# A transformer block's attention output written with heads and queries exchanged, in place of a query split that exchanged them

## What is computed

```
x = x + layernorm(attention(layernorm(x)))     # 32 query heads, 8 key/value heads of 128, causal
x = x + layernorm(ffn(layernorm(x)))           # silu(g) * u, inner width 1792

# attention, for key/value head k and its 4 query heads g
scores = einsum('bskgd,btkd->bkgst', qh, kh) * scale
scores = where(causal, scores, min)
probs  = softmax(scores)
attn   = einsum('bkgst,btkd->bskgd', probs, vh).reshape(B, S, 32 * 128)
out    = attn @ w_dense.T
```

## Time and profile before

| | |
|---|---|
| median of 3 runs | 1152.4 us |
| the profiled execution, its own time | 1152.48 us |
| its span, first to last instruction | 1150.7 us |
| mean granted TensorE clock | 0.991 |
| busy in the span: PE, DVE, ACT, POOL | 1100.3, 858.5, 665.7, 827.9 us |
| DMA | 227.9 MB |

### The profile page before, as it was taken

How to read it: one execution, slowest core, us unless ns; L and a number is a source line. 1 busy time by engine, 2 the same in 40 slices (tenths; PEclk the granted TensorE clock), 3 DMA queues, 4 the chain that set the end, 5 groups by cost and what they waited for, 6 DMA issues and landing times.

```text
span 1150.7 us, 16547 instructions
## 1 busy us (share of the span) xinstructions
PE 1100.3 (96%) x5134; PEld 912.6 (79%) x5134; DVE 858.5 (75%) x1706; ACT 665.7 (58%) x1231; POOL 827.9 (72%) x821
## 2 busy tenths in 40 slices
PE   8999999999999999998999999999999899999997
PEld 7888888888888787777877777877888677888885
DVE  5545455557999898899889998888677866566666
ACT  6432324239897687777777877865577532222224
POOL 7844447449979879798789699897865656666545
PEclk9999999999999999999999999999999999999999
DMA  6444565445997898797887988976210033333422
GB/s 222 125 169 146 183 203 185 148 124 195 328 349 264 287 308 303 271 321 238 288 299 241 317 317 268 331 272 214 100 65 1 14 120 105 116 102 99 119 66 96
DMA packets 163536, 227.86 MB, mean 198 GB/s; under 512 B 37760, under 2 KB 126464, under 8 KB 158592
## 3 DMA queue, kind: packets, MB, share of 16 engines
q1 hardware_dynamic: 163456, 226.88, 59.4%
HBM read 130.50 MB, written 96.34 MB: 197 GB/s over the span
## 4 chain that ended last, share of the span: by engine, by line
PE 51%; POOL 16%; DVE 11%; DMA 11%; ACT 5%; issue 5%; SPq 1%; DVEq 0%; POOLq 0%; ACTq 0%
PE psOY L1598 14%; PE psS L1598 14%; PE psT L1598 12%; PE psOY L1735 5%; PE psOY L1750 4%; POOL pT_lo L673 4%; DMA p_scr_short<-probs_short 3%; POOL probs_long L733 3%; DMA p_scr_long<-probs_long 3%; POOL qT_lo L673 3%; DMA squares_long<-p_scr_long 2%; POOL probs_short L733 2%; DVE pT_lo L1254 2%; PE psT L1716 2%; DVE squares_long L1341 1%
## 5 line engine op out<-in xcount | busy, mean ns | idle before, releaser
L1048 ACT ACTIVATE probs_long<-probs_long,negmax 128x896 f32<-128x896 f32 (+9 forms) x124 | 122.2, 987 | 25.1 <-DVE negmax L1322 24.5
L733 POOL TENSOR_SCALAR probs_long<-probs_long,rsum 128x768 f32<-128x768 f32 (+9 forms) x98 | 104.0, 1068 | 35.5 <-DVE rsum L1329 35.2
L673 POOL TENSOR_TENSOR pT_lo<-squares_long,pT_hi 128x896 fp32r<-128x896 f32 (+3 forms) x47 | 105.8, 2257 | 16.3 <-ACT pT_hi L1043 16.3
L1341 DVE STREAM_TRANSPOSE squares_long<-squares_long 128x1792 f32<-128x1792 f32 (+3 forms) x54 | 101.7, 1886 | 17.5 <-DMA squares_long<-p_scr_long 17.4
L1750 PE MATMUL psOY<-wd_hi,oT_hi 128*128 128x512 f32 x256 | 105.7, 413 | 8.8 <-DVE oT_lo L1254 7.7
L673 POOL TENSOR_TENSOR qT_lo<-q_raw,qT_hi 128x512 fp32r<-128x512 f32 x64 | 102.6, 1604 | 11.6 <-ACT qT_hi L1032 11.6
L800 POOL TENSOR_SCALAR hidden<-mask,hr,hs 128x128 f32<-128x128 f32 x112 | 50.4, 459 | 80.9 <-DVE hr L1419 78.7
L1735 PE MATMUL psOY<-pT_hi,v_hi 128*128 128x512 f32 x222 | 89.9, 405 | 15.9 <-POOL pT_lo L673 10.0
L1750 PE MATMUL psOY<-wd_lo,oT_hi 128*128 128x512 f32 x256 | 101.5, 397 | 0.0
L1750 PE MATMUL psOY<-wd_hi,oT_lo 128*128 128x512 f32 x256 | 101.5, 396 | 0.0
L1598 PE MATMUL psS<-kT_hi,qT_hi 128*128 128x512 f32 (+5 forms) x280 | 98.6, 352 | 2.9 <-DVE negmax L1322 1.9
(11 more groups left out here) (214 smaller groups left out, 3386.8 us busy)
## 6 DMA issues: line engine op xcount, KB each, us to landing
q_raw<-q_scr SPq DMA_DIRECT2D x64, 256.0 KB, 4.7
p_scr_long<-probs_long SPq DMA_DIRECT2D x14, 896.0 KB, 7.0
squares_long<-p_scr_long SPq DMA_DIRECT2D x14, 896.0 KB, 5.7
p_scr_long<-probs_long SPq DMA_DIRECT2D x12, 1024.0 KB, 5.9
squares_long<-p_scr_long SPq DMA_DIRECT2D x12, 1024.0 KB, 6.5
p_scr_long<-probs_long SPq DMA_DIRECT2D x14, 768.0 KB, 4.9
squares_long<-p_scr_long SPq DMA_DIRECT2D x14, 768.0 KB, 5.1
raw<-in_w_qk SPq DMA_DIRECT2D x10, 1024.0 KB, 6.4
```

What stands on the lines that cost most here:

```text
L673: return nc.gpsimd.tensor_tensor(dst, source, hi.bitcast(F32), ALU.subtract)
L733: nc.gpsimd.tensor_scalar(row, row, rsum[:, column(t, u)], 1.0, ALU.mult, ALU.mult).then_inc(p_ready[lane(t)], 1)
L1048: nc.scalar.activation(row, row, ACT.Exp, bias=negmax[:, column(t, u)], scale=-1.0, accum_out=lsum[:, column(t, u)]).then_inc(e_done[lane( ...
L1341: nc.vector.transpose(rows, rows).then_inc(swap_turned[c], 1)
```

## The change

For exchanged tiles, the query split no longer reorders: `from_units(qT) <- by_head(q_raw)` for every tile. In an exchanged tile's unit the row is now head-major, partition 32b + q, the exchange makes it (a, b, s) with q = 4s + a, and psO comes out so. The copy of the output undoes what concerns the heads (`turned_rows`) and leaves the tokens of a unit in the order (a, s) in place of (s, a). Tiles that are not exchanged must bring their tokens into the same order; a copy with that many dimensions is written as four, one for each head.

So the rows of `y` and `x1` are permuted tokens. `tokens_of` gives the matching rows in DRAM, for one unit at a time: the loads of x and the stores of the result become four transfers each. The means of x, which DVE holds by tokens in order, go through a DRAM tensor `m_scr` and come back permuted in `xmv`. The mask of the exchanged tiles (`band`) is copied from the other mask. All five letter strings are new; in each only the order differs (of PE's the first line is shown).

```diff
-    PE_WEAVE = ("pspsppssvvvvsppsyysppysppyvppssvspspvvppvvvbbsbsbvbssyybyyvvvssbyyyybssvvvvvvvbbssyvyyyvssbvybvbyvbvvyyv"
+    PE_WEAVE = ("ppspspssvvvvppsspspypypvsppssysppsyvvpsspvvbbvvvbbssyyyyvvvsbbsyybbyybsbsvvvvvvvssyvybyyvbbssbvvvyvyyvyv"
...
-        def queries_in(tile, t):
+        def turned_rows(t):
 
             if away(t):
-                return tile[:].rearrange("p (u q b) -> p u q b", u=HG, b=HG)
-            return from_units(tile)
-
-        def queries_of(tile, t):
-            return tile[:].rearrange("p (b u q) -> p u q b", u=HG, b=HG) if away(t) else by_head(tile)
+                tiles = [u[:].rearrange("p (b w s) -> p b w s", b=HG, s=TURN_ROWS) for u in oT]
+                return [(psO.rearrange("p (w b s) -> p b w s", b=HG, s=TURN_ROWS), *tiles)]
+            banks, tiles = psO.rearrange("p (u b s a) -> p b u a s", u=HG, b=HG, a=HG), [
+                u[:].rearrange("p (b u a s) -> p b u a s", b=HG, u=HG, a=HG) for u in oT]
+            return [(banks[:, h], *[u[:, h] for u in tiles]) for h in range(HG)]
+
+        def tokens_of(t, i, u):
+
+            return t[i * P + u * SPAN:i * P + (u + 1) * SPAN, :].rearrange("(s a) d -> a s d", a=HG)
...
+                    sp.dma_start(m_scr, mv[:].rearrange("p i k -> p (i k)")).then_inc(mean_out, 16)
...
+                    sp.wait_ge(mean_out, 16)
+                    for u in range(HG):
+                        sp.dma_start(xmv[u * SPAN:(u + 1) * SPAN].rearrange("p i k -> p (i k)"), tokens_of(m_scr, 0, u)
+                                     ).then_inc(mean_in, 16)
...
-                        sp.dma_start(x1[:, i, :], x[i * P:(i + 1) * P, :]).then_inc(x_in[i], 16)
+                        for u in range(HG):
+                            sp.dma_start(x1[u * SPAN:(u + 1) * SPAN, i, :], tokens_of(x, i, u)).then_inc(x_in[i], 16)
...
-                sp.dma_start(out[i * P:(i + 1) * P, :], x1[:, i, :]).then_inc(out_done, 16)
-            sp.wait_ge(out_done, 16 * NT)
+                for u in range(HG):
+                    sp.dma_start(tokens_of(out, i, u), x1[u * SPAN:(u + 1) * SPAN, i, :]).then_inc(out_done, 16)
+            sp.wait_ge(out_done, 16 * HG * NT)
...
-                hi, lo = (queries_in(u, t) for u in qT[t % 3])
-                low(lo, queries_of(q_raw[t % 2], t), hi).then_inc(q_lo, 1)
+                hi, lo = (from_units(u) for u in qT[t % 3])
+                low(lo, by_head(q_raw[t % 2]), hi).then_inc(q_lo, 1)
...
-                nc.scalar.copy(queries_in(qT[t % 3][0], t), queries_of(q_raw[t % 2], t)).then_inc(q_hi, 1)
+                nc.scalar.copy(from_units(qT[t % 3][0]), by_head(q_raw[t % 2])).then_inc(q_hi, 1)
...
-                    nc.scalar.copy(by_head(oT[0]), from_units(psO)).then_inc(o_hi, 1)
+                    for bank, hi, _ in turned_rows(args[0]):
+                        last = nc.scalar.copy(hi, bank)
+                    last.then_inc(o_hi, 1)
...
-                    lo_part(by_head(oT[1]), from_units(psO), by_head(oT[0])).then_inc(o_done, 1)
+                    for bank, hi, lo in turned_rows(args[0]):
+                        last = lo_part(lo, bank, hi)
+                    last.then_inc(o_done, 1)
```

More of the change, by code:

```diff
@@ L74, in sandwich_kernel @@
     SPAN = P // HG
+    TURN_ROWS = SPAN // HG
     AWAY = range(3, T - NT)
@@ new lines, in sandwich_kernel @@
+    ACT_WEAVE = ("pppepeeqeppoqppeepprepqeqpeenpeepnpqpffroeffeeqeqohhffqfrfeeeqkeorhhffofeefnqkeeqnohffhqffoeekqeeknohnhf"
+             "ofqfqfkeekeerohrhffoqffeeqkerehohffreeoffkneenqffohfqfheeoqnkeekqohnhqoeffkeffeekqohfhfroffeqreeeqkhohff"
+             "freeofkrnqeeqnffohhfqfoekeqeeknohnffhfoeeqfekkeqrohhrffreeoqffkeerohhqffeefonfqkqeeffnohhffoqeekknoheeqf"
+             "nfhffoeeqeekkqohhofrfffeerqrkeeorqhffhffoqeeekeqnffohhnqoffeekkonqeenhohqfefefqfkekeohffffrhoqrerekreefo"
+             "fqhfhfqeeokqneeffnffohhqoeefkqfnkeeohnfheofqerkkeerohhqoferefffeeqkohqhqoekeereohhoqeeeppoppepopqpppeppe"
+             "eepaeeoppqpcpeeopiapppeepjeqaepcppceieeopepjepoppippapeppeeeopapcpepejppipepaoppcxcijxoixgaxjcgjxaigcjxi"
+             "gtgxjgxtgdttdgdtd")
@@ new lines, in sandwich_kernel @@
+    POOL_WEAVE = ("bnnqnnqdnqrnnnnqnqdmrmmmnnqnnqllmmmmqrnnnnqllmmnmmqqnlmqmrmmqnnkldlmmqmmqnnknnrllqrmmmmnnnndlqlmmmmnrnqm"
+             "qmlmrmqnnkqllqdmmmmnnnnqklrlrmmmmnnqnnqdmmllmmnqqrnrlmqmmmqnknldmlmnmnmqkqnnrlmmlmqmnnrdnnqlmmlmmnqrqnmm"
+             "mmrlqnklndmqmlmmnqnknndlmlrmqmmrqnnnnqmmllmmrqrqnnlmmmmqnkqdnllmmmmqnnknnlmmlmmrrqnnqnnmmqllmmnqqrrmmnmm"
+             "qldnkqnlmlmnqmnmrknnllqrmmnnmmnqrnllqqlnndrnnndnnqnununnzynqunnaqnnyxuynnaunnxannnnuqxnynnnaynnxnnyaaxwx"
+             "ygawgyxagwgxgwgwgwg")
@@ L297, in sandwich_kernel @@
         st = small("st", [P, 2, 6])
-        mv = small("mv", [P, NT, 2])
+        mv, xmv = small("mv", [P, NT, 2]), small("xmv", [P, NT, 2])
         rstd, rstd1, nmean = (small(n, [P, NT]) for n in ("rstd", "rstd1", "nmean"))
@@ L333, in sandwich_kernel @@
         LENGTHS = ("short", "long")
-        swap_out = [[sem(f"swap_out_{n}{k}") for k in range(HG)] for n in LENGTHS]
-        swap_in = [[sem(f"swap_in_{n}{k}") for k in range(HG)] for n in LENGTHS]
+        swap_out = [[sem(f"swap_out_{n}{k}") for k in range(HG // 2)] for n in LENGTHS]
+        swap_in = [[sem(f"swap_in_{n}{k}") for k in range(HG // 2)] for n in LENGTHS]
         swap_turned, swap_hi, swap_lo, swap_lo_pool = ([sem(f"{what}_{n}") for n in LENGTHS] for what in
                                                        ("swap_turned", "swap_hi", "swap_lo", "swap_lo_pool"))
+        mean_out, mean_in = sem("mean_out"), sem("mean_in")
         wd_in, ffn_in, out_done, ffn_free = sem("wd_in"), sem("ffn_in"), sem("out_done"), sem("ffn_free")
@@ L498, in swap_away @@
                     sp.wait_ge(swap_in[c][k], 16 * (count - 2))
-                by_quarter = kept(t, k).rearrange("(b p x) -> p b x", b=HG, p=P)
-                sp.dma_start(by_quarter, rows.rearrange("p (b x) -> p b x", b=HG)).then_inc(swap_out[c][k], 16)
+                scratch, width = kept(t, k)
+                by_quarter = scratch.rearrange("(b p x) -> p b x", b=HG, p=P)
+                sp.dma_start(by_quarter[:, :, 0:width], rows.rearrange("p (b x) -> p b x", b=HG)).then_inc(swap_out[c][k], 16)
             def swap_back(t, k):
@@ L509, in swap_back @@
                         sp.wait_ge(swap_lo_pool[c], low_count(earlier, POOL_LOW, end))
-                sp.dma_start(rows, kept(t, k).rearrange("(p x) -> p x", p=P)).then_inc(swap_in[c][k], 16)
+                scratch, _ = kept(t, k)
+                sp.dma_start(rows, scratch.rearrange("(p x) -> p x", p=P)).then_inc(swap_in[c][k], 16)
             def store(kind, n, tile, done):
@@ L953, in _ @@
                     corner = band[:, HG - 1, 2 * P - SPAN:2 * P]
-                    nc.gpsimd.affine_select(out=corner, in_=corner, compare_op=ALU.is_ge, fill=NEG, base=0,
-                                            pattern=[[-HG, SPAN]], channel_multiplier=1).then_inc(band_ready, 1)
+                    nc.gpsimd.tensor_scalar(corner, mask[:, S - SPAN:S], 1.0, 1.0, ALU.mult, ALU.mult).then_inc(band_ready, 1)
                 elif kind == "zeros":
```

62 lines of the change are left out of this document (27 added, 35 removed).

## The result

The changed kernel takes **1137.1 us** (median of 4 runs, 1132.85 to 1137.74) against 1152.2 for the kernel before (4 runs): a ratio of 0.9856, 95% interval 0.9823 to 0.989, or 13 to 20 us less. The prediction was 1154 with a range from 1146. It missed, and by a part that it had given nothing: the new orders. (One run of the kernel before, beside e13 to e16, took 1542.3 us at a granted clock of 0.655; it is left out of all comparisons.)

A forecast was written before the change was run, and what follows sets the result against it. TensorE's own work was taken to bound the kernel, leaving its idle time to win (31.8 us in the attention stage). Query split -9, output's copy +1.5, stores +9 sum to +1.5 on 1152.48, so 1154 us, range 1146 to 1161.5.

The forecast's parts named there:

- The orders: New order of the engines' instructions: nothing in a row tells what they are worth, so no term in the sum.
- a bad new order: Risk named, without a size: a new order that leaves TensorE waiting where it didn't would make the prediction wrong.
- an attention stage that gains over 15 us: Sign named beforehand that would show the prediction wrong; the attention stage was expected to gain about 9 us.
- The query split: Attention stage, 53 exchanged tiles: splitting without reordering frees ACT 27.9 us and POOL 19.0; taken as -9 us, bounds 0 and -19.
- The output's copy: Copy from PSUM: nothing for exchanged tiles, four instructions per engine for 11 others; taken as +1.5 us, bounds 0 and 16.
- The stores: End of kernel: four transfers per tile, each quarter on four DMA engines, 2.6 us per tile; taken as +9 us.
- The loads of x: 32 issues on SP from 821.5, holding four DMA engines 21 us in the worse case; covered, so no cost.
- the margin of 2 to 5 us: Time by which the x loads were expected to stay covered before the cast at 847.1, in the worse case.
- DVE sets the pace: Rival: the change gives DVE nothing between 250 and 850; -2 in the attention stage, sum +8.5, 1161 us, chance 0.20.
- More is won: Rival: in the attention stage whatever POOL is given back shows up, -16 there, sum -5.5, 1147 us, chance 0.17.
- Spread stores: Rival: the final stores use all DMA engines, costing +4.7 us in place of +9; 1149.6 us, chance 0.15.
- dear reads: Rival: strided reads in the output's copy are dear, half of 16 us exposed, +8 for +1.5; 1160 us, chance 0.08.

The follow-up runs named there:

- e13: Kernel before with its own orders, from tile 20 on POOL subtracts only two of four parts of each low part of the exchanged probabilities: 1132.6 us.
- e16: Kernel before with the new orders, from tile 20 on DVE's low parts of the exchanged probabilities halved: 1123.0 us.
- e2: Kernel before with the five letter strings of the changed kernel, so the new orders alone: 1127.4 us (ratio 0.9798).
- e1: Changed kernel with the five letter strings of the kernel before, so the new form without its new orders: 1154.4 us (ratio 1.0023).
- e7: Changed kernel with each quarter of the result stored as 32 plain rows of 512 in place of 4 by 8 by 512: 1129.5 us (0.982).
- e8: Changed kernel with SP's 32 loads of x moved behind the last two query loads: 1130.1 us (0.9816).
- e11: Changed kernel with POOL's low part of the queries in the reordering form of before for the 53 exchanged tiles, ACT's cast new: 1140.6 us.

## Why the prediction was wrong

**The orders: this step failed.** The sum had "the orders are new and nothing in a row tells what they are worth", and entered zero, with no rival for it. They were worth -24.6 us (e2). The rows had the room: TensorE lost 53.7 us between 250 and 800, and the earlier trace rows put 26.4 us of waits in front of the values, which the order of five lists decides. I listed a bad new order as a risk; for a good one there was only the sign "an attention stage that gains over 15 us", without a cause or a chance.

**The query split: right in size.** -9, measured under the old orders by e1: -9.9 of loss, -8.8 at the last product. In the changed kernel, busy time of qT_hi on ACT, then of qT_lo on POOL, answering to the earlier trace rows:

```profile
262.00:740.00 478.00, 32.52 (x53) 1.00 0.88 305
...
262.00:740.00 478.00, 72.36 (x53) 1.00 0.88 305
```

0.614 and 1.365 us each (0.62 and 1.30 predicted), so POOL was given 15.5 us and not 19.0. The way to the -9 is not confirmed: it was worked out from the chain's pieces of qT_lo and qT_hi, and the clock was not in it, while the 6.4 us at half clock that the kernel before has and e1 has not are among the 9.9. That the sum of the two effects came to -9 may be luck. Under the new orders the split is worth about 5 us by TensorE's loss: less is left to win once TensorE no longer waits.

**The output's copy: right.** Answering to the earlier trace rows:

```profile
L1273 DVE TENSOR_TENSOR oT_lo<-psOY,oT_hi 128x512 fp32r<-128x512 f32 x53 | 36.2, 683 | 11.6 <-ACT oT_hi L1202 11.3
L1202 ACT CAST oT_hi<-psOY 128x512 fp32r<-128x512 f32 x53 | 30.9, 582 | 46.2 <-PE psOY L1757 46.1
L1273 DVE TENSOR_TENSOR oT_lo<-psOY,oT_hi 128x128 fp32r<-128x128 f32 x44 | 9.7, 282 | 4.1 <-ACT oT_hi L1202 4.0
L1202 ACT CAST oT_hi<-psOY 128x128 fp32r<-128x128 f32 x44 | 8.6, 285 | 7.1 <-PE psOY L1757 7.1
```

Runs of 8 cost nothing on either engine. Steps of four elements cost DVE nothing (282 against 285 ns) and ACT at most 26 ns a piece, so the upper bound of 16 us was far off. e1 as a whole came out 1.8 us above the kernel before by the spans, where the sum had +1.5.

**The stores: right, a little small.** +9 predicted, +10.5 in the changed kernel, and e7 shows the mechanism: four engines carry each quarter. That the issue of this pattern takes 0.66 us and not 0.47 was not in the sum, and costs little beside them.

**The loads of x: half right.** 21 us on four engines, measured 21.74; under the old orders they are covered, as I said: e1 has no wait for a query load there. But the cover was read from the old orders and the changed kernel has others, in which the margin of 2 to 5 us was gone: some 6 us (e8). It was on my list of what could go wrong, with no price.

**The rivals.** "DVE sets the pace" was refuted by e1 (-9.9 of loss). "More is won" had the sign, but its cause, POOL's freed time, is worth 3.5 us by the medians (e11). "Spread stores" and "dear reads" fell. (In the chances a tenth of 0.40 is 0.04, not 0.05, and the range ends 1 and 0.5 us outside the centres 1147 and 1161; neither matters.)

## What to carry to other kernels

When a change comes with a new order, it is two changes: run the old form with the new order and the new form with the old one before saying what either is worth. Here the form alone was worth nothing and the order 25 us. A forecast should give a new order a range as wide as the stalls of the bounding engine that an order can reach, in the direction of gain too.

A wait that goes away with the improvement need not be its cause: the 21 us of DVE's waits for the exchange vanished with the new orders, and removing them by themselves won 4.5. Halve the suspected cost, under the old and the new order, and compare the two gains. Then look in the trace whether only that cost moved: here cutting POOL's pieces shortened DVE's too.

Transfers whose pattern has a small outermost count are slow twice: in themselves, and for what stands behind them in the issuing queue.
